# Turning the convolution's tiles back by DMA transposes, with ACT splitting, joining and issuing, in place of transposes on PE

## What is computed

```python
# mixer: k = v = ctx_2048, q = layernorm(x), 64 heads of 8 channels, L = 1024
kv = einsum('bhil,bhjl->bijhl', k_, v_)
y = irfft(rfft(kv, n=2 * L) * rfft(ssm_kernel, n=2 * L), n=2 * L)[..., :L]
out = einsum('bijhl,bhil->bjhl', y + kv * D, q_)
x = x + tanh(g_xattn[0]) * out
# feed-forward on layernorm(x): bf16, weights and inputs quantised in blocks of 32
h = mx_linear(mx_layernorm(bf16_round(inputs), ln_w, ln_b), W1, b1)
x = x + tanh(g_ffn[0]) * bf16_round(residual + mx_linear(mx_gelu(h), W2, b2))
```

## Time and profile before

| what | value |
|---|---|
| time, median of 3 runs | 1971.58 us (1971.25 to 1971.68) |
| the profiled execution, its own time | 1971.53 us |
| its span, first to last instruction | 1969.8 us |
| PE busy over the span | 1875.5 us (95%) |
| DVE busy | 1654.8 us (84%) |
| ACT busy | 949.6 us (48%) |
| POOL busy | 872.0 us (44%) |
| mean granted clock of PE | 0.983 |

### The profile page before, as it was taken

One profiled execution on the slowest core, in us unless ns is written; L12 is line 12 of the kernel. 1 busy time (PEld: TensorE's weight loads), 2 busy tenths in 40 slices (PEclk: granted clock), 3 DMA queues, 4 the chain that ended last, 5 costly groups with the idle time before them and its releaser, 6 DMA issues. The chain is left out here.

```text
span 1969.8 us, 28534 instructions
## 1 busy us (share of the span) xinstructions
PE 1875.5 (95%) x11384; PEld 1474.7 (75%) x11432; DVE 1654.8 (84%) x1919; ACT 949.6 (48%) x1227; POOL 872.0 (44%) x645
## 2 busy tenths in 40 slices
PE   6999999999999999999966997999999999999998
PEld 5988888898888888898854665666777766666773
DVE  5889988999888888898789798899888888898843
ACT  5555556555555655555503542444455444444440
POOL 3888788787889889999930000000000000000000
PEclk9999999999999999999978998999999999999999
DMA  6665556677665665767558312221222121221112
GB/s 236 217 208 169 179 163 202 218 274 245 221 209 174 215 208 175 237 189 220 166 202 312 123 39 75 76 75 54 65 76 76 65 68 51 75 76 44 54 43 75
DMA packets 163749, 287.95 MB, mean 146 GB/s; under 512 B 105952, under 2 KB 105952, under 8 KB 155424
## 3 DMA queue, kind: packets, MB, share of 16 engines
q1 hardware_dynamic: 163616, 286.12, 44.2%
HBM read 218.91 MB, written 42.53 MB: 133 GB/s over the span
## 5 line engine op out<-in xcount | busy, mean ns | idle before, releaser
L328 PE MATMUL y_ps<-kk_hi,slab 128*128 128x352 f32 (+6 forms) x3328 | 892.7, 352 | 28.9 <-DMA slab<-taps_scratch 18.1
L328 PEld LDWEIGHTS y_ps<-kk_hi,slab 128*128 128x128 f32 x3328 | 596.7, 190 | 98.1 <-issue 29.8
L328 PE MATMUL y_ps<-kk_lo,slab 128*128 128x512 f32 (+6 forms) x1664 | 582.3, 350 | 0.0
L985 PE MATMUL acc_ps<-w_T,arena 128*128 128x512 bf16 x2000 | 439.5, 379 | 2.5
L970 PE MATMUL l_ps<-f_xq_T,w_T 128*128 128x256 bf16 x3584 | 398.3, 274 | 15.4 <-ACT arena L1031 10.7
L970 PEld LDWEIGHTS l_ps<-f_xq_T,w_T 128*128 128x128 bf16 x3584 | 352.6, 98 | 61.9 <-ACT arena L1031 11.2
L985 PEld LDWEIGHTS acc_ps<-w_T,arena 128*128 128x128 bf16 x2048 | 200.4, 98 | 238.5
L328 PEld LDWEIGHTS y_ps<-kk_lo,slab 128*128 128x128 f32 x1664 | 315.8, 190 | 34.6
L765 POOL TENSOR_TENSOR terms<-terms 128x768 f32<-128x768 f32 x127 | 334.5, 2634 | 10.0
L1031 ACT ACTIVATE arena<-l_ps,f_b 128x256 bf16<-128x256 f32 x512 | 213.4, 474 | 252.3 <-PE l_ps L970 247.4
L1280 POOL TENSOR_TENSOR f_rstd<-f_var_eps,f_neg_half 128x1 f32<-128x1 f32 x28 | 15.4, 549 | 697.7 <-DVE f_var_eps L1090 697.7
(11 more groups left out here) (130 smaller groups left out, 1880.8 us busy)
## 6 DMA issues: line engine op xcount, KB each, us to landing
slab<-taps_scratch SPq DMA_DIRECT2D x128, 512.0 KB, 4.9
arena<-in_w_m SPq DMA_DIRECT2D x32, 1024.0 KB, 6.2
arena<-x_scratch SPq DMA_DIRECT2D x60, 512.0 KB, 3.8
k_ext<-in_ctx_e SPq DMA_DIRECT2D x64, 384.0 KB, 3.4
arena<-in_w SPq DMA_DIRECT2D x18, 1024.0 KB, 6.5
x_tile<-in_x_t SPq DMA_DIRECT2D x32, 512.0 KB, 4.9
out_t<-arena SPq DMA_DIRECT2D x32, 512.0 KB, 2.6
x_scratch<-x SPq DMA_DIRECT2D x31, 512.0 KB, 3.3
```

The source lines that it names most:

```text
L328: mm = nc.tensor.matmul(y_ps[:, y_base + begin:y_base + end], slab[s][:, half, d * P:(d + 1) * P], kk_part[s][:, begin - d * PAIR:end - d ...
L985: mm = nc.tensor.matmul(acc_ps[s][:, c * 512:(c + 1) * 512], hidden[g % 2][:, k, s * P:(s + 1) * P], w2_T[:, k, c * 512:(c + 1) * 512], st ...
```

## The change

The transposes of `mixed` leave PE, but for the last tile (`turn_last`). In their place, for tiles 0 to 30:

- ACT's `split_mixed(t)` copies the tile `mixed` into its 16-bit halves in `xn_halves` and issues a DMA transpose into `q_halves`; both buffers are shared with the turning of q, and the waits keep the two uses apart.
- ACT's `merge_back(t)` joins the halves from `q_halves` into `x1[t % 2]`, in the order of x; DVE's `residual(t)` then adds x in place.
- `split_mixed(t - 1)` stands in the odd head of tile `t`, behind `take_q`; `merge_back(t - 2)` in the even head, behind `high_half(h + 1)` and ahead of `ln_apply`.
- DVE's `residual(t - 2)` stands in the even head of tile `t`, in the place between `make_kk(h + 1)` and `times_q(h, 0)`, where it stood for `t - 1` in the odd head.
- All DMA transposes of the mixer are issued by ACT: that of q right behind its split, and the four early ones.
- SP's stores and loads of x move to the even head. The early statistics and the weight maxima move by one head. POOL waits for `mixed_split` before it overwrites `mixed[t % 2]`.

The diff, cut to its core:

```diff
-    maxima_heads = list(range(6)) + list(range(7, early_heads + 5, 2))
-    maxima_heads += [early_heads + 5 + 2 * n // 3 for n in range(2 * W_TILES - len(maxima_heads))]
+    maxima_heads = list(range(6)) + list(range(8, early_heads + 6, 2))
+    maxima_heads += [early_heads + 6 + 2 * n // 3 for n in range(2 * W_TILES - len(maxima_heads))]
...  SP
-                if h % TILE_HEADS == 1 and t + 1 < tiles:
-                    turn_halves(t + 1)
-                if h % TILE_HEADS == 1 and t >= 1:
-                    store_x1(t - 1)
-                    if t + 3 < tiles:
-                        load_x(t + 3)
-                if h >= 9 and h % 4 == 1 and (h - 9) // 4 < EARLY:
-                    turn_early((h - 9) // 4)
+                if h % TILE_HEADS == 0 and t >= 2:
+                    store_x1(t - 2)
+                    if t + 2 < tiles:
+                        load_x(t + 2)
...  PE
-                    if h % TILE_HEADS == 1 and i == 0 and t >= 1:
-                        turn_back(t - 1)
-            turn_back(tiles - 1)
+            turn_last()
...  ACT, split_halves(t)
+                if t >= 3:
+                    act.wait_ge(mixed_turned, 16 * (t - 2))
                 nc.scalar.copy(xn_halves, xn[:].bitcast(I16).rearrange("p (l h) -> p h l", h=2)).then_inc(halves_ready, 1)
+                act.wait_ge(halves_ready, t)
+                if t >= 3:
+                    act.wait_ge(back_merged, t - 2)
+                act.dma_start(q_halves, xn_halves.rearrange("p h l -> p (h l)"), transpose=True).then_inc(halves_turned, 16)
+
+            def split_mixed(t):
+                act.wait_ge(sums_ready, 2 * TILE_HEADS * (t + 1))
+                act.wait_ge(halves_turned, 16 * min(t + 2, tiles - 1))
+                nc.scalar.copy(xn_halves, mixed[t % 2][:].rearrange("p n c -> p (n c)").bitcast(I16)
+                               .rearrange("p (l h) -> p h l", h=2)).then_inc(mixed_split, 1)
+                act.wait_ge(mixed_split, t + 1)
+                act.wait_ge(q_ready, min(t + 3, tiles))
+                act.dma_start(q_halves, xn_halves.rearrange("p h l -> p (h l)"), transpose=True).then_inc(mixed_turned, 16)
+
+            def merge_back(t):
+                act.wait_ge(mixed_turned, 16 * (t + 1))
+                if t >= 2:
+                    act.wait_ge(x1_stored[t % 2], 16 * (t // 2))
+                if t % 2 == 0 and 1 <= t // 2 <= EARLY:
+                    act.wait_ge(e_norm, t // 2)
+                words = view(x1[t % 2].bitcast(I16), 0, [(2, L // QB), (2 * L // QB, QB), (1, 2)])
+                source = view(taps_hi_all.bitcast(I16), 0, [(QB, L // QB), (1, QB), (LB * P, 2)])
+                nc.scalar.copy(words, source).then_inc(back_merged, 1)
...  ACT, the order
                 if t + 1 < tiles:
                     if h % TILE_HEADS == 0:
+                        if t >= 2:
+                            merge_back(t - 2)
                         ln_apply(t + 1)
                         split_halves(t + 1)
                     else:
                         take_q(t + 1)
+                        if t >= 1:
+                            split_mixed(t - 1)
                         if t + 2 < tiles:
                             ln_stats(t + 2)
+                elif h % TILE_HEADS == 0:
+                    merge_back(t - 2)
+                else:
+                    split_mixed(t - 1)
+                if h >= 10 and h % 4 == 2 and (h - 10) // 4 < EARLY:
+                    turn_early((h - 10) // 4)
...
+            merge_back(tiles - 2)
...  DVE
             def residual(t):
-                dve.wait_ge(back_ready, t + 1)
-                if 2 <= t < tiles - 1:
-                    dve.wait_ge(x1_stored[t % 2], 16 * (t // 2))
+                dve.wait_ge(back_merged, t + 1)
+                nc.vector.tensor_tensor(x1[t % 2][:], x1[t % 2][:], x_tile[:, t % X_SLOTS, :], ALU.add).then_inc(x1_ready, 1)
...
-                if h % TILE_HEADS == 1 and t >= 1:
-                    residual(t - 1)
+                if h % TILE_HEADS == 0 and t >= 2:
+                    residual(t - 2)
                 times_q(h, 0)
...
+            residual(tiles - 2)
             last_part()
             first_ints(dve)
-            residual(tiles - 1)
+            last_residual()
...  POOL, sum_part
+                if t >= 2 and part == 0:
+                    pool.wait_ge(mixed_split, t - 1)
```

More of the change, by code:

```diff
@@ L184, in mixer_block @@
         halves_ready, halves_turned = sem("halves_ready"), sem("halves_turned")
+        mixed_split, mixed_turned, back_merged = sem("mixed_split"), sem("mixed_turned"), sem("back_merged")
         back_ready, x1_ready = sem("back_ready"), sem("x1_ready")
@@ L228, in store_w2 @@
                 sp.dma_start(w2_q[j], w2_raw[j % 3][:, 0:L].bitcast(BF16)).then_inc(done, 16)
[L230 to L239, removed]
             def store_x1(t):
@@ L306, in _ @@
                 sp.wait_ge(turned, 16 * EARLY // 2)
+            store_x1(tiles - 2)
             for parity in range(2):
@@ L342, in spread_inverses @@
                 pe.wait_ge(inv_repeated, r + 1)
-                pe.wait_ge(x1_ready, spread_heads[r] // TILE_HEADS - 1)
+                if r == 0:
+                    pe.wait_ge(q_ready, 1)
+                else:
+                    pe.wait_ge(inv_kept, r)
                 for n in range(LB):
@@ L346, in spread_inverses, with turn_last @@
                 mm.then_inc(inv_spread, 1)
[L348 to L357, removed]
+            def turn_last():
+                t = tiles - 1
+                pe.wait_ge(sums_ready, 2 * heads - 1)
+                pe.wait_ge(last_sums, 1)
+                pe.wait_ge(inv_kept, len(spread_heads))
                 for n in range(LB):
@@ L674, in residual, with last_residual @@
             def residual(t):
-                dve.wait_ge(back_ready, t + 1)
-                if 2 <= t < tiles - 1:
-                    dve.wait_ge(x1_stored[t % 2], 16 * (t // 2))
-                if t % 2 == 0 and 1 <= t // 2 <= EARLY:
-                    dve.wait_ge(e_norm, t // 2)
-                out = x1_last if t == tiles - 1 else x1[t % 2][:]
-                nc.vector.tensor_tensor(out.rearrange("p (i k) -> p i k", i=QB),
+                dve.wait_ge(back_merged, t + 1)
+                nc.vector.tensor_tensor(x1[t % 2][:], x1[t % 2][:], x_tile[:, t % X_SLOTS, :], ALU.add).then_inc(x1_ready, 1)
+            def last_residual():
+                t = tiles - 1
+                dve.wait_ge(back_ready, 1)
+                nc.vector.tensor_tensor(x1_last.rearrange("p (i k) -> p i k", i=QB),
                                         view(turn_ps, 0, [(1, QB), (QB, L // QB)]),
@@ L698, in _ @@
                     low_half(h + 1)
-                if h >= 3 and h % 4 == 3 and h // 4 < EARLY:
-                    early_statistics(h // 4)
-                if h >= 5 and h % 4 == 1 and h // 4 - 1 < EARLY:
+                if h >= 4 and h % 4 == 0 and h // 4 - 1 < EARLY:
+                    early_statistics(h // 4 - 1)
+                if h >= 6 and h % 4 == 2 and h // 4 - 1 < EARLY:
                     early_second_statistics(h // 4 - 1)
-                if h >= 6 and h % 4 == 2 and h // 4 - 1 < EARLY:
+                if h >= 7 and h % 4 == 3 and h // 4 - 1 < EARLY:
                     early_input(h // 4 - 1)
-                if h >= 8 and h % 4 == 0 and h // 4 - 2 < EARLY:
+                if h >= 9 and h % 4 == 1 and h // 4 - 2 < EARLY:
                     early_quantise(h // 4 - 2)
@@ L776, in _ @@
                     inv_sqrt(h // TILE_HEADS + 1)
-                if h >= 4 and h % 4 == 0 and h // 4 - 1 < EARLY:
+                if h >= 5 and h % 4 == 1 and h // 4 - 1 < EARLY:
                     early_rstd(h // 4 - 1)
-                if h >= 6 and h % 4 == 2 and h // 4 - 1 < EARLY:
+                if h >= 7 and h % 4 == 3 and h // 4 - 1 < EARLY:
                     early_second_rstd(h // 4 - 1)
```

7 lines of the change are left out of this document (6 added, 1 removed).

## The result

The changed kernel takes 2117.6 us in the median (2111.6 to 2122.1, four runs), the kernel before 1971.6 beside it: 1.0735 times the time, 95% interval 1.0701 to 1.0770. The profiled execution of the changed kernel took 2111.59 us with a span of 2109.8; what follows is read against its own span and against the 1969.8 of before.

The account below looks back on a forecast made before the run. PE bound the kernel at 30.76 us a pair; afterwards DVE would: 34.4 + 0.5 (ACT late) + 0.4 (clock) = 35.3, +138 us over 30 pairs and 1.2 for residual(30), so 1971.6 + 139 = 2110 us; range 2065 to 2190.

Parts of the forecast that it names:

- The stall by the place of the wait: Even heads, DVE before the residual: waits for ACT's three steps, 3.4 us, and the merge, 2.4: 5.8 us a pair.
- The rival at 3.5 to 4.5 us: ACT's merge pays for its long steps: 1.1 to 2.1 us a pair more, 2145 to 2175 us; chance 0.14.
- ACT's lateness: Odd heads with little weight work: ACT ends late and lengthens DVE's stall, 0.5 us a pair on the mean.
- the landing: Transpose of mixed lands about 14 to 15 us after make_kk, before the merge begins at 17 or later: no wait.
- The residual: DVE's residual in the even head costs the same as before, 1.20 us, with the same count of elements.
- an issue holds ACT as long as SP, 3.17 us: Each transpose issue, two a tile, assumed to hold ACT's queue 3.17 us, SP's median; bound from below nothing.
- The odd head: DVE before low_half(h+1): 1.6 us idle for high_half, plus 0.4 us for PE's clock, a pair.
- The clock: PE's gap of five microseconds a pair brings the half clock: some 1.5 us of PE time, 0.4 us counted.
- What leaves PE: 31 of 32 turn_back calls go from PE, at most 31 x 1.04 = 32 us; PE then needs 29.3 a pair.
- POOL, SP, the DMA engines: POOL's work fits in the longer pair; SP and extra DMA traffic put at 0, bounds -2 and +10 us.
- The rest of the program: residual(30), now after the last heads, adds 1.2 us.
- The other side: Rival: PE stays the bound and heads speed up by the transposes, 1940 us, if stall under 2.1 us; chance 0.03.

Follow-up runs that it names:

- in the shade of `high_half`: Changed kernel with residual(t - 2) in the odd head between make_kk(h + 1) and times_q(h, 0), transposes issued by SP: 1982.1 us, ratio 1.0050.
- the run with SP issuing: Changed kernel with all DMA transposes issued by SP again, other engines' order unchanged: 2090.7 us, ratio 1.0609.
- the run with the filled gap: Changed kernel with 32 more PE transposes of the identity behind the last stretch of each of 26 even heads: 2107.0 us, ratio 1.0692.
- the kernel with the transposes added on SP: Kernel before with one transpose of eight in turn_back for tiles 0 to 30, plus 30 more DMA transposes on SP: 1955.3 us, ratio 0.9921.
- the two kernels with SP held back: Changed kernel, ACT issuing, SP's transfers held back: residual behind low_half(h + 1), 2070.6 us; residual in the odd head before times_q(h, 0), 2056.0 us.

## Why the prediction was right, point by point

- **The time.** 2110 us forecast, 2117.6 measured; against the profiled execution the forecast misses by 2 us. A pair was put at 35.3 us and took 35.6.
- **The stall by the place of the wait.** Forecast 5.8 us by order alone; where nothing else is late the trace has 5.47 to 5.50 us. The merge was put at 2.4 us and took 2.15, near the 2.3 worked out from `take_q`. The rival at 3.5 to 4.5 us falls. The Trainium skill's rule of the 16-byte lines (SBUF — State Buffer, Door 1) is hardly borne out for this copy of halves: writing pairs 128 bytes apart costs 2.15 us for 2048 against 1.90 for the split. For 32-bit words `ln_apply` of the earlier trace rows agrees with it.
- **The rest of the stall.** It sums to 183.0 us over 30 heads, of which 30 x 5.48 = 164 is the order. In the trace ACT began `copy_k` late in seven even heads, 12.4 us in all, and in three heads the merge waited for its transpose (1.94, 4.39 and 0.63 us). The prediction had 0.5 x 30 = 15 us for ACT's lateness and nothing for the landing. The sum is right (6.2 a pair against 5.8 + 0.5), and its parts are off by a few us each.
- **The residual.** Put at its old 1.20 us, it took 1.23 in the changed kernel, where POOL stands idle beside it in all of the first 30 tiles. The prediction gave the equal count of elements as the reason, but it is a matter of the place: in the shade of `high_half` the same instruction took 2.7 to 3.8 us in each of the first 29 tiles.
- **What the issue costs ACT.** The step "an issue holds ACT as long as SP, 3.17 us" was right in kind and wrong in size: 5.37 us in the median for q, 1.81 for `mixed`. The two errors nearly cancel in the sum of a pair (7.2 against 6.3). That it was worth little at this place (27 us by the run with SP issuing) and much once the stall was gone (62 us) was not foreseen; the sum gave ACT one number for both.
- **The odd head.** Forecast 1.6 us for `kk_hi` and 0.4 for the clock; measured 12.5 + 54.3 us, 2.3 a pair, nearly all put down to PE and not to `kk_hi`, since PE came so late with its result that `kk_hi` was ready by then. The sum was right, the split between the two was not.
- **The clock.** Put at 1.5 us of PE's time a pair, of which 0.4 would count, 12 us in all. PE's busy time in the window rose by 24.5 us (893.99 to 918.53) although some 30 us of transposes had left it, so the clock costs PE some 55 us, 1.9 a pair. What counts of it is 3 to 11 us by the run with the filled gap, which filled 26 heads; that is of the size forecast, and not measured closer.
- **What leaves PE.** Named as 32 us at most and not part of the sum, as DVE is the bound afterwards. Alone it is worth 12.7 us.
- **POOL, SP, the DMA engines.** Put at 0; 30 added transposes on SP cost nothing to be seen. The rest of the program, put at +1.2 us, came out 3 us shorter; no run was made on that.
- **The other side.** It was to decide at a stall under 2.1 us. Where the stall is taken away and ACT freed, the kernel is at 1990 and 1982 us, not at 1940.

What stays open: the 27 us between the kernel with the transposes added on SP (1955) and the one with the residual in the shade (1982) are, by the account of DVE above, mostly the residual's longer time beside POOL; no run takes it out to see what comes back. Whether it is the operand in PSUM that let the old residual run beside POOL, or the order of its elements, was not tested either.

## What to carry to other kernels

When an operation is moved to another engine, look first at where its consumer stands in its own engine's order, and at what the producer must do first: here the data were ready a head early, and DVE still waited 5.5 us each time, since ACT's merge was queued behind three steps that waited for DVE itself. The time of such a wait is the sum of the rows in between, less the slack at that place, and it can be read in the trace of before. After taking one such wait away, measure again before counting the gain: the next one, here ACT held by its DMA issues, had been hidden behind it. And when a move changes where an operand lies or which engine works beside it, compare the busy time too: the waits alone would not have shown the 54 us that DVE's residual lost beside POOL.

## What the runs showed of the hardware

The time for which the issue of a DMA transpose holds its engine goes with what has been sent shortly before. The same instruction took from 1.33 to 7.4 us on ACT in the changed kernel. Here is SP in the three microseconds or so before a long one, and then the long one and a short one on ACT:

```profile
847.10 0.32 SPq L236 DMA_DIRECT2D x_scratch<-x  x1
847.46 0.43 SPq L200 DMA_DIRECT2D x_tile<-in_x_t  x1
847.94 0.78 SPq L224 DMA_DIRECT2D arena<-in_w  x1
848.77 0.49 SPq L229 DMA_DIRECT2D w_scratch<-arena  x1
849.30 0.91 SPq L208 DMA_DIRECT2D slab<-taps_scratch  x2
```

```profile
850.22 7.39 ACTq L396 DMA_TRANSPOSE taps_hi<-taps  x1
...
867.08 1.90 ACTq L410 DMA_TRANSPOSE taps_hi<-taps  x1
```

Ahead of the long issue SP sent six transfers; ahead of the short one none (its next slabs left at 868.23). Over the 62 issues of that trace, sorted by what SP had sent within 3 us, the median is 1.8 us with nothing sent (13 issues), 3.8 with 1 MB (20), 4.9 with 1.5 or 2 (13), 5.8 with 2.5 or 3 (15), and the one with 3.5 MB took 7.0. Three microseconds are not the whole reach: in the two kernels with SP held back the longest issues (9.6 and 11.3 us) had their transfers 4 to 8 us ahead, while none of the 60 issues with nothing sent for 8 us took more than 3.1 us. The two kernels with SP held back move the long issues from one transpose to the other, which is what a cause in the transfers ahead would do; that it is the amount in bytes and not the number of transfers was not tested. The Trainium skill (DMA: Bandwidth & Descriptors, "Issuing engines are not separate DMA queues") says that DMAs from several engines run on the same 16 DMA engines and interleave, and that the time to initiate one is usually small beside the DMA. The first agrees with this; for these transposes the second does not hold, with medians of 5.37 and 1.81 us of issue against 8.8 and 7.2 us from issue to landing.

Of PE's clock: in the changed kernel PE's gap of 3.03 us before 885.79 was followed by about three microseconds at a granted clock of 0.50, the lower of the two levels, and then by 1.00 again:

```profile
887.00:888.00 1.00, 1.00 (x5) 1.00 (x5) 1.00 (x1) 0.00 (x0) 1.00 (x1) 0.50 1.05 430
...
890.00:891.00 1.00, 1.00 (x8) 1.00 (x8) 1.00 (x2) 0.00 (x0) 1.00 (x1) 1.00 1.24 234
```

Not every such gap has it: one of 2.28 us before 918.95 was followed by 1.00 throughout.

Of DVE beside POOL: instructions of DVE that read one operand from PSUM kept their time, and two whose operands all lie in SBUF did not. The larger part of `make_kk`, which reads `k_ps`, took 1.74 to 1.75 us in every head after 60 us, in the kernel before and in the one with the shade; `low_half`, all in SBUF, took 2.55 to 3.68 us in the kernel before, and the new residual 1.21 to 3.75 in the one with the shade.
